# Fewer gathers in the edge pass of a graph kernel: two groups without edges left out, 30 factor gathers and a loop of further ones moved to later blocks

## The reference, cut to what matters

```
# layer 0: a max over the edges of each source node, added to x, then layer norm
h   = relu(concat(x[src], x[dst] - x[src]) @ W + b)
x   = layernorm(x + max(segment_max(h, src), 0))

# layer 1: a polynomial of degree 5 in the normalised adjacency
D    = deg ** -0.5                       # deg: how often a node is a dst; 0 where deg is 0
norm = D[src] * D[dst]
coef = softmax(W2 @ relu(W1 @ [mean(x, 0), mean(x), std(x), N, E] + b1) + b2)
tx, result = x, coef[0] * x
for k in 1..5:
    tx     = segment_sum(norm * tx[dst], src)
    result = result + coef[k] * tx
x = layernorm(x + result)
```

## Time and profile before

| | us |
|---|---|
| runs | 3283.93, 3303.49 (median), 3313.57 |
| the profiled execution, first to last instruction | 3301.7 |
| edge pass | 1314 to 2054 |
| mixing | 2054 to 2066 |
| sum pass H5 | 2066 to 2170 |
| busy over the span | VectorE 79%, GpSimd 66%, ScalarE 61%, TensorE 55% |

### The profile page before, as it was taken

One profiled execution on the slowest core, in us unless ns is written; L12 is line 12 of the kernel. 1 busy time (PEld: TensorE's weight loads), 2 busy tenths in 40 slices (PEclk: granted clock), 3 DMA queues, 4 the chain that ended last, 5 costly groups with the idle time before them and its releaser, 6 DMA issues. The chain is left out here.

```text
span 3301.7 us, 66681 instructions
## 1 busy us (share of the span) xinstructions
PE 1810.2 (55%) x9465; PEld 1080.2 (33%) x9465; DVE 2592.2 (79%) x12088; ACT 2029.5 (61%) x4485; POOL 2193.2 (66%) x2267
## 2 busy tenths in 40 slices
PE   6888655538888886888888885333342332000000
PEld 4666444425555553444444442111111111000000
DVE  7888899999999997798989997555566666555554
ACT  6999777726666664688878884345555500444443
POOL 5775477027777776577777775766666665777776
PEclk9999899979999998588878896555555555555555
DMA  3311244317777776588878886766667733222221
GB/s 117 109 46 20 72 110 110 87 60 204 203 203 204 204 204 160 126 211 209 213 196 212 213 213 138 178 160 176 179 171 187 185 92 81 70 70 70 74 73 53
DMA packets 736782, 467.28 MB, mean 142 GB/s; under 512 B 411287, under 2 KB 622546, under 8 KB 736728
## 3 DMA queue, kind: packets, MB, share of 16 engines
q1 hardware_dynamic: 636084, 321.23, 36.4%
q0 software_dynamic: 75296, 92.22, 12.7%
q10 hardware_dynamic: 25348, 53.33, 5.2%
HBM read 271.38 MB, written 197.86 MB: 142 GB/s over the span
## 5 line engine op out<-in xcount | busy, mean ns | idle before, releaser
L1642 POOL DMA_INDIRECT rows_H<-tab,at_H x424 | 407.6, 961 | 211.2 <-DVE at_H L1695 108.9
L943 POOL DMA_INDIRECT rec<-edge_x,pos x392 | 411.9, 1051 | 163.3 <-issue 159.1
L1145 POOL DMA_INDIRECT rows_M<-x_ext,at_M x400 | 378.3, 946 | 161.6 <-issue 109.8
L1917 POOL DMA_INDIRECT out_x<-res_L,to_L x384 | 374.0, 974 | 118.9 <-issue 103.5
L1663 ACT ACTIVATE node_H<-node_H,mean,M2n 125x64 f32<-125x64 f32 x800 | 273.6, 426 | 256.5 <-issue 151.1
L1803 PE MATMUL zT_H<-ident,z_H 128*64 128x128 f32 x496 | 150.6, 408 | 441.9 <-issue 346.3
L853 PE MATMUL gps<-table,hiT 125*128 125x400 bf16 x1568 | 299.8, 334 | 93.1 <-DVE picked L787 92.0
L391 POOL DMA_INDIRECT edge_x<-in_x,x_at x220 | 216.7, 985 | 85.3 <-issue 66.4
L538 POOL DMA_INDIRECT edge_x<-in_x,x_at x172 | 164.5, 957 | 104.2 <-issue 52.1
L444 PE MATMUL cps<-ohc,ohp 128*125 128x400 bf16 x784 | 200.1, 337 | 54.7 <-ACT ohd L409 54.7
L591 PE MATMUL aps<-ohc_f,ohp_f 128*125 128x400 bf16 x784 | 156.8, 344 | 127.5 <-DVE ohp_f L512 127.5
(11 more groups left out here) (319 smaller groups left out, 6008.7 us busy)
## 6 DMA issues: line engine op xcount, KB each, us to landing
tab<-given_M SPq DMA_DIRECT2D x98, 384.0 KB
hibc_f<-dst_hi_rows SPq DMA_DIRECT2D x98, 256.0 KB
hibc<-hi_rows SPq DMA_DIRECT2D x98, 256.0 KB
srcbc<-src_rows SPq DMA_DIRECT2D x98, 256.0 KB
tab<-given_M SPq DMA_DIRECT2D x98, 256.0 KB
own<-given_M SPq DMA_DIRECT2D x98, 256.0 KB
own_L<-own SPq DMA_DIRECT2D x192, 128.0 KB
x_ext<-wide SPq DMA_DIRECT2D x100, 241.5 KB
```

The costliest lines, as they stand in the source:

```text
L943: pool.indirect_dma_start(out=d.rec, out_offset=bass.IndirectOffsetOnAxis(ap=pos[:, s, j:j + 1], axis=0), in_=edge_x[:, i + s * (EB // 2), ...
L1145: pool.indirect_dma_start(out=rows[:, s, j, :], out_offset=None, in_=d.x_ext, in_offset=bass.IndirectOffsetOnAxis(ap=at[:, s, j:j + 1], ax ...
L1642: pool.indirect_dma_start(out=rows[:, s, j, :], out_offset=None, in_=gather, in_offset=bass.IndirectOffsetOnAxis(ap=at[:, s, j:j + 1], axi ...
L1917: pool.indirect_dma_start(out=d.out, out_offset=bass.IndirectOffsetOnAxis(ap=to[:, s, j:j + 1], axis=0), in_=res[:, s, j, :], in_offset=No ...
```

## The change

Three things. The edge pass runs `target`, `mark`, `far_moments`, `load_ids` and `gather` for groups 0 to 97 alone, and two memsets fill `nd` and `to` of the last two groups; the pipeline's loop ends at group 96 (LOOPED) and more periods are written out. GpSimd issues 108 factor gathers (EDGE_D) in the edge pass, spread so that the last comes with group 97, and 30 more in the mixing block, where GpSimd had nothing. The loop for tiles from 138 on stands at the end of GpSimd's stream in H5. Because of that, the scaling of `k.Ds` goes from H5 to H4.

```diff
+EDGE_D = 108
 def pipeline(eng, groups, ns, *steps):
     most = max(lag for lag, _, _ in steps)
+    end = max(lag + last for lag, last, _ in steps) + 1
...
-    for t in range(groups, groups + most):
+    for t in range(groups, end):
         period(t)
...
 def edge_pass(nc, d, k):
     NS = 4
     LAST = NG - 3
+    LOOPED = NG - NS
...
         def _(pool):
-            pool.memset(d_got[:], 1.0)
             pool.memset(k.Ds[:], 1e6).then_inc(d_blank, 1)
             pool.wait_ge(d_blank, 1)
             asked = 0
-            for g in range(NG):
+            for g in range(LAST + 1):
                 gather(g)
-                upto = max(0, (g - 8) * D_GT * 4 // 9)
+                upto = min(EDGE_D, max(0, (g - 8) * EDGE_D // (LAST - 8)))
                 for t in range(asked, upto):
                     factor(t)
                 asked = max(asked, upto)
-            for t in range(asked, EARLY_D):
-                factor(t)
-            pool.wait_ge(d_all, EARLY_D * 16)
-            pool.wait_ge(told, NG)
-            with pool.Fori(0, pool.value_load(k.rounds[0:1, 7:8], ...)) as i:
-                ...    # moved to sum_pass, see below
+            pool.wait_ge(d_all, EDGE_D * 16)
+            pool.wait_ge(told, LAST + 1)
...
+            dve.memset(k.nd[:, (LAST + 1) * GT:, :], 0.0)
+            dve.memset(k.to[:, (LAST + 1) * GT:], int(FAR))
...
-            pipeline(dve, NG, NS, (1, NG - 1, target), (3, NG - 1, mark), ..., (3, NG - 1, far_moments), ...)
+            pipeline(dve, LOOPED, NS, (1, LAST, target), (3, LAST, mark), ..., (3, LAST, far_moments), ...)
...
 def mixing(nc, d, k):
...
+        @block.gpsimd
+        def _(pool):
+            for t in range(EDGE_D, EARLY_D):
+                pool.indirect_dma_start(
+                    out=k.Ds[:, t:t + 1], out_offset=None, in_=d.factor,
+                    in_offset=bass.IndirectOffsetOnAxis(ap=k.to[:, t:t + 1], axis=0),
+                    bounds_check=N - 1, oob_is_err=False,
+                ).then_inc(d_rest, 16)
+            pool.wait_ge(d_rest, (EARLY_D - EDGE_D) * 16)
...
 def sum_pass(nc, d, k, name, coef, gather, chunks, store=None, late=None):
...                                  # behind the gathers of the pass, in GpSimd's stream
+            if first:
+                pool.memset(d_got[:], 1.0).then_inc(d_blank, 1)
+                pool.wait_ge(d_blank, 1)
+                with pool.Fori(0, pool.value_load(k.rounds[0:1, 7:8], ...)) as i:
+                    issued, landed, at_tile = settle(...)
+                    pool.tensor_copy(d_at[:], k.to[:, ds(at_tile, D_GT)]).then_inc(d_ready, 1)
+                    pool.wait_ge(k.begun, 1)
+                    pool.wait_ge(d_ready, issued)
+                    for j in range(D_GT):
+                        pool.indirect_dma_start(out=d_got[:, j:j + 1], ..., in_=d.factor, ...).then_inc(d_in, 16)
+                    pool.wait_ge(d_in, landed)
+                    pool.tensor_copy(k.Ds[:, ds(at_tile, D_GT)], d_got[:]).then_inc(d_kept, 1)
+                    pool.wait_ge(d_kept, issued)
...
-                link(dve.tensor_scalar(k.Ds[:, 0:used], k.Ds[:, 0:used], k.coef[:, 6:7], None, ALU.mult))
+            def scale_factors():     # run once in H4, early in the pass
+                dve.tensor_scalar(k.Ds[:, 0:used], k.Ds[:, 0:used], k.coef[:, 6:7], None, ALU.mult).then_inc(scaled, 1)
+                dve.wait_ge(scaled, 1)
```

More of the change, by code:

```diff
@@ L1053, in edge_pass @@
         dev_done, mch = sem("dev_done_M"), sem("mch_M")
-        d_all, d_ready, d_in, d_kept = (sem(f"{nm}_M") for nm in ("d_all", "d_ready", "d_in", "d_kept"))
+        d_all = sem("d_all_M")
         block = scope.enter_context(nc.Block())
@@ L1304, in _ @@
             act.wait_ge(begun, 1)
-            pipeline(act, NG, NS, (4, LAST, follow), (4, LAST, penalty), (4, LAST, far), (3, LAST, turned),
+            pipeline(act, LOOPED, NS, (4, LAST, follow), (4, LAST, penalty), (4, LAST, far), (3, LAST, turned),
                      (7, LAST, make_rows), (4, LAST, pair_turned), (6, LAST, give_sums), (3, NG, deviation))
@@ L1409, in shifts @@
                                   ).then_inc(idle_ready[s], 1)
[L1411 to L1412 removed]
+            pipeline(dve, LOOPED, NS, (1, LAST, target), (3, LAST, mark), (4, NG, inverse), (6, LAST, first_layer), (4, NG, shifts),
+                     (4, LAST, far_factors), (3, LAST, far_moments), (6, LAST, row_moments), (3, NG, chunk_moments),
                      (3, NG, moments), (4, LAST, running_max), (4, LAST, running_sum))
@@ L1416, in _ @@
             all_squares(dve)
-            dve.wait_ge(told, NG)
+            dve.wait_ge(told, LAST + 1)
             link(dve.memset(k.qs[:], 0.0))
@@ L1608, in sum_pass @@
             dev_done, made = sem("dev_done_H5"), sem("made_H5")
+            d_at, d_got = sb("d_at", [P, D_GT], U32), sb("d_got", [P, D_GT])
+            d_blank, d_ready, d_in, d_kept = (sem(f"{nm}_H5") for nm in ("d_blank", "d_ready", "d_in", "d_kept"))
+        scaling = coef == 4
+        scaled = sem(f"scaled_{name}")
         stores = [t[:, C:2 * C] for t in d.tab] if first else [] if final else [store]
@@ L1645, in _ @@
                         ).then_inc(gathered[s], 16)
+            if first:
+                pool.memset(d_got[:], 1.0).then_inc(d_blank, 1)
+                pool.wait_ge(d_blank, 1)
+                with pool.Fori(0, pool.value_load(k.rounds[0:1, 7:8], min_val=1, max_val=(NT - EARLY_D) // D_GT)) as i:
+                    issued, landed, at_tile = settle(pool, k, i + 1, i * (16 * D_GT) + 16 * D_GT, i * D_GT + EARLY_D)
+                    pool.tensor_copy(d_at[:], k.to[:, ds(at_tile, D_GT)]).then_inc(d_ready, 1)
+                    pool.wait_ge(k.begun, 1)
+                    pool.wait_ge(d_ready, issued)
+                    for j in range(D_GT):
+                        pool.indirect_dma_start(
+                            out=d_got[:, j:j + 1], out_offset=None, in_=d.factor,
+                            in_offset=bass.IndirectOffsetOnAxis(ap=d_at[:, j:j + 1], axis=0),
+                            bounds_check=N - 1, oob_is_err=False,
+                        ).then_inc(d_in, 16)
+                    pool.wait_ge(d_in, landed)
+                    pool.tensor_copy(k.Ds[:, ds(at_tile, D_GT)], d_got[:]).then_inc(d_kept, 1)
+                    pool.wait_ge(d_kept, issued)
         @block.scalar
@@ L1784, in late_shifts @@
                 dve.scalar_tensor_tensor(l_shift[:], l_total[:], -0.5, l_rstd[:], ALU.mult, ALU.mult).then_inc(l_shift_done, 1)
-            extra = dict(early=late_moments, then=late_shifts) if late else {}
+            extra = dict(early=late_moments, then=late_shifts) if late else dict(early=scale_factors) if scaling else {}
             fetch(0, 0)
```

11 lines of the change are left out of this document (5 added, 6 removed).

## The result

The changed kernel takes 3315.27 us (median of 20 runs, 3303.77 to 3329.41), the kernel before 3297.11 us in the 20 runs beside it (3283.93 to 3314.66). The ratio is 1.0043 with a 95% interval of 1.0027 to 1.0059: **slower by 14 us (9 to 19)**. The direction was forecast and the time lies in the range, but the move was to be +27.4 us, and half of it did not come. That 3315 us lies in a range of 3311 to 3347 is owed to the room left there for two rivals, not to the sum. The two profiled executions agree with the runs: their spans are 3316.2 and 3301.7 us, 14.5 us apart, and the span of the changed kernel lies 1.7 us under its execution's time of 3317.87.

A forecast was written before the change was run, and what follows sets the result against it. VectorE at the 2.4 GHz level and TensorE at 1.2 GHz, not GpSimd, were taken to bound the edge pass. Terms -12.0 + 35.4 + 4.0 = +27.4 us on the 3301.7 us span gave a median of 3331 us, range 3311 to 3347.

The forecast's parts named there:

- two rivals: Edge pass: GpSimd sets the pace, 3317 us, chance 0.08; the clock falls differently, 3311 to 3351 us, chance 0.24.
- Step 1: Edge pass, steady part: fewer factor gathers between gathers, 1.21 per group instead of 1.33; costed at 0, ends 0 and -14 us.
- the far end, -14 us: Edge pass, fewer factor gathers: the gain over 89 groups if GpSimd set the pace.
- the clock falls differently: Rival, steady part: four half-clock groups more or less, 2.5 us each, move it 10 us either way; chance 0.24.
- distance still 6.37 at full clock: Sign for the steady part: two successive `target`s stay 6.37 us apart at full clock, as before the change.
- Step 2: Edge pass's end: groups 98 and 99 not gathered, so waits and VectorE work go; -7.0 us, ends 5.2 and 8 us.
- Step 3: Edge pass's end: GpSimd and its drain done early, engines meet 0.3 us after VectorE; 5.0 us saved.
- Step 4: Mixing: 30 factor gathers with nothing beside them, 39.6 us plus 6.6 us of drain; +35.4 us, ends +31 and +38.
- Step 5: H5: the loop behind the last gather ends after SyncE's last store; +4.0 us, ends 0 and +7.3.
- Step 6: H4: scaling moved from H5, done while VectorE waits for the pass's first gathers; 0, ends -1 and +1 us.
- The second road of the GpSimd rival: Edge pass: GpSimd's gathers and VectorE block each other over a shared port pair; same price, 3317 us, joint chance 0.08.
- the GpSimd rival: Edge pass: GpSimd, 97% booked, sets the pace, so fewer factor gathers give -14 us, 3317 us; chance 0.08 with its second road.

The follow-up runs named there:

- e3: The changed kernel with none of the 108 factor gathers of the edge pass, mixing's kept: 3322.31 us, ratio 1.0070 to the kernel before.
- e9: The kernel before with all 138 factor gathers of the edge pass left out, the loop of further ones kept: 3284.93 us, ratio 0.9971.
- e2: The changed kernel with the edge pass's factor gathers at the old rate, 4 in 3 groups: 3319.05 us, ratio 1.0048 to the kernel before.
- e8: The kernel before with groups 98 and 99 not gathered, new loop bounds, memsets, and all 138 factor gathers pulled forward in the edge pass: 3279.70 us, ratio 0.9933.
- e6: The kernel before with only groups 98 and 99 not gathered, the new loop bounds and the two memsets: 3285.77 us, ratio 0.9951.
- e4: The changed kernel with mixing's 30 factor gathers moved behind group 97 in the edge pass: 3285.97 us, ratio 0.9960 to the kernel before.
- e5: The kernel before, unedited, run again for a second trace: 3294.75 us, ratio 0.9986.
- f4: Second profile, one execution, of the kernel before with 108 factor gathers by group 97 and 30 behind group 99: 3305.29 us.
- e1: The changed kernel with the 30 factor gathers of mixing left out: 3283.84 us, ratio 0.9954 to the kernel before.
- e7: The changed kernel with groups 98 and 99 gathered again and the old loop bounds: 3327.76 us, ratio 1.0072 to the kernel before.
- e12: The changed kernel, unedited, run again for a second trace: 3309.06 us, ratio 1.0039 to the kernel before.

## Why the prediction was right or wrong

**Step 1, the step that failed: "I cost it at nothing, because VectorE or TensorE sets the pace".** The steady part got 13 us shorter in the profiled pair and 15 on the means of three. The forecast of +27.4 was off by 13 us, and this part alone is that much; the errors of the other steps cancel. It is the size of the far end, -14 us, but not for its reason; that the two agree is luck. The argument itself held in the changed kernel: GpSimd sets no pace. With no factor gathers in e3 the part took 545.7 us, and in the 78 groups of the window the changed kernel's marks never waited for a gather:

```profile
L1317 DVE TENSOR_TENSOR rows_M<-ids_M,behind_M x78: 148/152/321, 1443.3 to 1966.8; 128x4 f32<-128x4 f32 x78
its engine sat idle before it (us, times) until:
who waited for it (us, times):
  PE zT_M L1205: 9.7, 22
  PEld zT_M L1205: 8.9, 14
```

What changed with it is the time at the 1.2 GHz level. At the higher level a group still takes 6.4 us in both kernels (median of the groups without a fall); groups of over 6.7 us were 42 of 80 before and 26 of 80 after. So this was the rival "the clock falls differently", which I had held for scatter with a mean of zero. Its price of 2.5 us a group was that of a group wholly at the lower level; 16 slow groups fewer gave 13 us, 0.8 us each, because most of them lie there only in part. Per microsecond at the lower level the price holds: 2.5 of 8.87 us are 0.28, and 58 us fewer at that level gave 13.1 us, 0.23. The shift comes with the changed kernel, as the three profiles and the clocks of all executions show. My test for it, "distance still 6.37 at full clock", was passed and did not see it: it asked for the duration of a group at one level, not for the share of groups at each.

Why the clock is held better stays open. The memsets alone, the new bounds with them, and the rate of factor gathers alone each came with some of it in single profiles, none with all. Nor is GpSimd's load ruled out as a part of it in the kernel before: without factor gathers (e9) the steady part took 549.7 us, 7 us under the mean of three, and the clock over ten whole executions was 0.762 against 0.759 beside them. It is no wait that a trace shows, and TensorE's work in a group is the same in both kernels. That the clock sets the pace here and not the pace the clock is argued from the earlier trace rows; no run shows it.

**Step 2, -7.0 forecast, -8.9 measured.** The waits for the repeated row's gathers are gone and the chain comes sooner, as said. It lies 0.9 us beyond the upper end of 8 us. The clock has a part in this: from `target` 97 to the chain it was 0.84 before and 0.98 after. With the new bounds and a clock of 0.95 to 0.99 the stretch took 31.5 to 31.6 us in five profiles, and 35.7 and 36.3 us at 0.81 and 0.82 (e2, e8). e6, at 0.85, took 33.7, which is 6.8 us less than before at nearly the same clock. So the forecast of 7.0 was about right. That the rest is clock is likely but not shown, since e4 took 33.6 us at 0.94 and e5, with the old bounds, 38.6 us at 0.73.

**Step 3, -5.0 forecast and measured.** GpSimd's DRAIN was over at 2002.3, 23 us before the chain ended, and the meeting came 0.3 us behind VectorE.

**Step 4, +35.4 forecast, +32.9 measured.** First bar 0.9 us in, pace 1.30, as said. The term that was mis-sized is the drain: 4.1 us from the end of the last bar (2066.92) to 2071.0, not 6.6. It is made of the landing, 1.5 us, and a DRAIN of 2.5 us. The two places that I had read 6.6 from were unlike this one: in the edge pass a copy and the end of a loop stood between the last gather and the DRAIN, and in H5 the DRAIN had begun before the last gather. The changed kernel's own edge pass shows how little the distance means: its DRAIN took 8.70 us and ended 14.0 us after its last gather's bar. What a DRAIN waits for stays open. The Trainium skill (Perfetto Trace Analysis, DMA Instruction - SWDGE) puts the end of such a bar at the last descriptor's writing and the data's movement behind it; the landing at 1.5 us agrees, and the page's rule leaves the DRAIN behind it out. By the page alone this step would have come to some 30 us, about as far under the measured 32.9 as mine lay over it.

**Step 5, +4.0 forecast, +4.2 measured,** GpSimd last instead of SyncE. Right by size and engine; the DRAIN behind the last copy was 6.19 us.

**Step 6, 0 forecast.** H4 to H1 are 3.6 us longer. They are 620.7 to 621.7 us in eight profiles with the old bounds, 623.1 in a ninth (f4), and 623.1 to 625.3 in all with the new ones, e6 and e8 included, which keep the scaling in H5. So it is not the scaling; some 3 us come with the new bounds, except that f4 has them too, and I have no cause for them.

**The second road of the GpSimd rival.** I wrote that nothing was seen of GpSimd's gathers and VectorE holding each other up. That was a misreading: the 1.76 us bar of the earlier trace rows was it, beside VectorE's whole-table operations, and e4 shows three such bars in a row. The Trainium skill (SBUF - State Buffer, section on the two separate sides) says that the port pair is an exclusive lock: a VectorE operation with two inputs in SBUF and a GpSimd operation that reads SBUF block each other, and whichever starts first keeps the pair to its end. The rows agree if a gather's read of its indices counts as such a read, which no run shows: in seven profiles 17 gathers of factors started with 0.3 us or more of a two-input operation still to run, and every one of them ended 0.86 to 0.87 us after that operation's end; gathers that started first, or beside the one-input reciprocal, were not slowed. VectorE itself lost nothing (0.99 us an operation beside gathers in e4, and 0.99 us in the changed kernel, where GpSimd was idle). In the steady part no gather's bar shows it, 947 ns in the mean against 946 before.

**The sum by ratios.** e1 says that mixing's gathers cost 29 us, the rest of the change gains 15 (0.9954). I had put the rest at -12.0 + 4.0 = -8.0. The missing 7 us are the steady part's gain less what H4 to H1 lost (-13.1 and +3.6 in the profiles), and with 6 us less for mixing they make the 13 between +27.4 and +14.

**The scatter of the kernel itself goes with the clock.** In 78 executions of the kernel before beside the experiments, mean clock (0.752 to 0.769) and time (3281 to 3314 us) go together with a correlation of -0.91. So the clock is worth tens of us in this kernel, the 29.6 us between three runs among them, and a change can move its mean: I should have asked for that before I gave the rival a mean of zero.

## What to carry to other kernels

Work is free only beside other work of the same block. Before you move it from under a chain, ask what stands beside it at its new place, and charge it with its own drain at that block's end. Where two engines set the pace in turn with the clock, compare the time at each level, and the mean clock of all executions, and not only a group's duration, with at least three profiles of each kernel: one pair gave 13 us here for a mean of 15, but kernels of like streams were up to 9 us apart.

## What the runs showed of the hardware

- The time from the end of the last indirect DMA's bar to the end of GpSimd's DRAIN is no constant: 4.1 us in mixing (DRAIN of 2493 ns, the same in e7 and e12), 5.4 us in e4, 8.3 us in H5 behind the loop (2170.4 to 2178.7), 14.0 us at the end of the changed kernel's edge pass (DRAIN of 8700 ns), 6.7 and 6.5 us in the two places of before.
- An indirect DMA that started while VectorE ran an operation with two whole tables as inputs ended 0.87 us after that operation (bars of 1.19 to 1.78 us in 17 cases); one that started just before such an operation, or beside a reciprocal of one table, kept its 1.00 us.
- The eight gathers that fetch one and the same row 1024 times took most of the 48.6% of the DMA engines' time for 743 packets, where 739 packets of other rows took 9.1%. The packets that carry the rows (2208 bytes) took 1666 ns in the mean there and 142 ns before; without these gathers the edge pass lost its last waits.
- The granted clock differed between kernels whose engines do the same work per group, 0.84 to 0.86 in three profiles of one and 0.89 to 0.90 in three of the other.
